# Reordered steps in the pair loop of a hyperbolic attention block: two accumulating transfers issued earlier, one MLP half later, the output add ahead of two PSUM copies

## The reference

```python
x = x + _L1_attn_ref(_layernorm(x, axis=-1), L1_attn_wq, L1_attn_wk, L1_attn_wv, L1_attn_wo)
x = x + _L1_ffn_ref(_layernorm(x, axis=-1), L1_ffn_w1, L1_ffn_b1, L1_ffn_w2, L1_ffn_b2)

# inside _L1_attn_ref, heads of width 8, c = 1
diff_sq = q_norm_sq + k_norm_sq - 2.0 * qk
denom = jnp.maximum((1.0 - c * q_norm_sq) * (1.0 - c * k_norm_sq), 1e-06)
dist = jnp.arccosh(jnp.maximum(1.0 + 2.0 * c * diff_sq / denom, 1.0))
attn = jax.nn.softmax(-dist, axis=-1)

# _L1_ffn_ref
h = jax.nn.relu(jnp.einsum('bsd,dw->bsw', x, w1) + b1)
return jnp.einsum('bsw,wd->bsd', h, w2) + b2
```

## Time and profile before

| | us |
|---|---|
| executions | 2479.14, 2481.09, 2484.28 |
| the profiled execution, its own time | 2479.14 |
| its span in the profile | 2477.0 |
| from the first sum of this stage (1364.0) to the end | 1113 |
| clock of TensorE, mean over the span | 0.879 of full |

### The profile page before, as it was taken

The page is one execution under the profiler, slowest core; times in us unless marked ns, Lnnn a source line. Parts: engine busy times, 40 slices in busy tenths (PEclk is TensorE's granted clock), DMA queues, the critical chain, the costliest instruction groups (busy, mean ns, idle before and its releaser), DMA issues. The chain is left out here.

```text
span 2477.0 us, 50064 instructions
## 1 busy us (share of the span) xinstructions
PE 2029.9 (82%) x15066; PEld 1513.2 (61%) x15066; DVE 1956.0 (79%) x5939; ACT 1767.8 (71%) x3085; POOL 1626.4 (66%) x1866
## 2 busy tenths in 40 slices
PE   4999999999999997999995766766777676776776
PEld 4677777777777766888883444544444444444445
DVE  4677776777767766787776899999999999999982
ACT  2666666666667654444422899999999999999985
POOL 2766676676667730000004989999999999999992
PEclk7999999999999997999996578788887878878886
DMA  5000000000000003534530776666766667766674
GB/s 141 1 2 2 2 1 2 2 1 2 1 2 1 1 1 75 120 84 91 117 70 10 136 136 125 121 120 127 140 129 119 119 122 140 139 118 120 119 133 79
DMA packets 81386, 184.22 MB, mean 74 GB/s; under 512 B 9478, under 2 KB 31529, under 8 KB 81194
## 3 DMA queue, kind: packets, MB, share of 16 engines
q0 software_dynamic: 36864, 134.23, 28.8%
q1 hardware_dynamic: 36010, 43.38, 7.8%
q10 hardware_dynamic: 8320, 4.19, 0.7%
HBM read 42.85 MB, written 4.72 MB: 19 GB/s over the span
## 5 line engine op out<-in xcount | busy, mean ns | idle before, releaser
L1551 POOL TENSOR_TENSOR spare<-spare,u 128x1024 f32<-128x1024 f32 x192 | 455.7, 2374 | 16.0
L542 ACT ACTIVATE prob<-s_ps,nmax 128x128 f32<-128x128 f32 (+1 forms) x1024 | 364.4, 432 | 132.2 <-DVE nmax L599 132.2
L599 DVE CUSTOM_DVE_ANT_0 s_ps<-s_ps,mask 128x128 f32<-128x128 f32 (+1 forms) x1024 | 340.7, 385 | 100.7 <-issue 76.4
L1373 PE MATMUL d_ps<-rowsT 28*128 28x256 f32 x1024 | 150.4, 371 | 252.2 <-DVE u L1631 251.6
L579 POOL TENSOR_TENSOR g_lo<-g_all,g_hi 128x512 fp32r<-128x512 f32 x256 | 329.2, 1286 | 21.4
L1627 DVE TENSOR_SCALAR u<-d_ps 128x1024 f32<-128x1024 f32 x256 | 312.0, 1219 | 37.8 <-PE i_ps L1373 36.7
L1631 DVE SCALAR_TENSOR_TENSOR u<-i_ps,u 128x1024 f32<-128x1024 f32 x256 | 313.5, 1225 | 13.2 <-DVE u L1627 0.5
L1373 PEld LDWEIGHTS d_ps<-rowsT 28*128 28x128 f32 x1024 | 97.0, 219 | 340.8 <-issue 329.3
L534 ACT COPY g_all<-g_ps 128x512 f32<-128x512 f32 x256 | 151.5, 592 | 162.6 <-PE g_ps L63 161.5
L1508 ACT ACTIVATE u<-u 128x1024 f32<-128x1024 f32 x256 | 256.6, 1056 | 0.3 <-DMA u<-spare 0.3
L1511 ACT ACTIVATE u<-u 128x1024 f32<-128x1024 f32 x256 | 255.7, 1051 | 0.0
(11 more groups left out here) (273 smaller groups left out, 5621.9 us busy)
## 6 DMA issues: line engine op xcount, KB each, us to landing
u<-spare POOLq DMA_DIRECT2D x256, 512.0 KB, 12.2
w_all<-w_rows SPq DMA_DIRECT2D x128, 256.0 KB, 5.9
x<-L_attn_x ACTq DMA_DIRECT2D x8, 512.0 KB, 13.9
y<-x SPq DMA_DIRECT2D x32, 128.0 KB, 9.9
wkqv<-L_attn_Wkqv SPq DMA_DIRECT2D x4, 528.0 KB, 8.8
gate_rows<-L_ffn_gate_proj SPq DMA_DIRECT2D x1, 512.0 KB, 14.3
up_rows<-L_ffn_up_proj SPq DMA_DIRECT2D x1, 512.0 KB, 11.4
down_cols<-L_ffn_down_proj SPq DMA_DIRECT2D x1, 512.0 KB, 13.2
```

The lines of the kernel that those rows point to most:

```text
L542: last = nc.scalar.activation(prob[:, kind, at, :].rearrange("p c n -> p (c n)"), s_ps[kind][:, at.start * P:at.stop * P], ACT.Exp, bias=n ...
L599: last = nc.vector.tensor_tensor_reduce(out=scores, in0=scores, in1=keep.mask[:, N - width:N], scale=-1.0, scalar=3.4e38, op0=ALU.add, op1 ...
L1373: last = nc.tensor.matmul(ps[:, e * W2 + j * N:e * W2 + (j + 1) * N], rowsT[at, slot(i, p), 1, j * P:(j + 1) * P], rowsT[at, slot(i, p), 0 ...
L1551: nc.gpsimd.tensor_tensor(extra, extra, pair, ALU.mult).then_inc(prod_done, 1)
```

## The change

Three moves; nothing is added or removed.

1. `SUMS_BEHIND`: GpSimd issues the sums of pairs 0 and 1 behind product 4, ahead of product 5, and the other six behind product 5 as before.
2. `HIDDEN_AT`: the first half of `pe_hidden` moves on TensorE from the end of p = 1 to p = 2, behind the pairs of p = 3 and ahead of the values. The second half keeps its place at p = 3.
3. VectorE, p = 1: `dve_y` stands ahead of the copies of rows 5 and 6 instead of behind them.

```diff
-    SUMS_BEHIND = {5: (0, 1, 2, 3, 4, 5, 6, 7)}
+    SUMS_BEHIND = {4: (0, 1), 5: (2, 3, 4, 5, 6, 7)}
...
-    HIDDEN_AT = (1, 3)
+    HIDDEN_AT = (2, 3)
...
-                        if four_before and p == HIDDEN_AT[1]:
-                            pe_hidden(pe, b - 4, 1, (b + 1) * (HP // 2))
+                        if four_before and p in HIDDEN_AT:
+                            if not one_after:
+                                pe.wait_ge(late_xT4_done, 1)
+                            pe_hidden(pe, b - 4, HIDDEN_AT.index(p), (b + 1) * (HP // 2))
                         if one_before and p in VALUES_AT:
                             pe_values(pe, b - 1, VALUES_AT.index(p), (i - 1) % TURN)
...
                         if five_before and p == 0:
                             pe_y(pe, b - 5, 2 * (b - 1))
-                        if four_before and p == HIDDEN_AT[0]:
-                            if not one_after:
-                                pe.wait_ge(late_xT4_done, 1)
-                            pe_hidden(pe, b - 4, 0, (b + 1) * (HP // 2))
...
                         dve_ratio(dve, b, p, i)
                         if p == 0 and three_before:
                             dve_residual(dve, b - 3)
+                        if p == 1 and five_before:
+                            dve_y(dve, b - 5)
                         for r in {0: (4,), 1: (5, 6), 2: (7,)}.get(p, ()):
                             copy_rows(dve, b, r, i)
-                        if p == 1 and five_before:
-                            dve_y(dve, b - 5)
```

## The result

The changed kernel takes 2571.15 us (median of 4 executions, 2565.5 to 2571.97), the kernel before 2480.11 us in the same comparison (4 executions, 2477.56 to 2484.28). The ratio is 1.0361 [1.0339, 1.0382]: 91 us slower. I had predicted 2510 us, with a range up to 2545. The profiled execution took 2562.97 us, its span is 2560.8.

What follows compares the result with a forecast made beforehand. VectorE's in-order program was taken as the chain, with ScalarE and GpSimd nearly full too. Move 3's 26.9 us plus Move 1's 1.8 in the tail made 28.7, so 2507.8 on the profiled execution, stated as 2510 us; range 2485 to 2545.

Steps and rivals of the forecast that it cites:

- So at full clock it costs the pairs nothing: TensorE ahead of the pairs of p = 4: 1.30 us of idle time covers the moved half's 1.03, leaving 0.27.
- 26.9 for the add: VectorE, `dve_y` ahead of the copies: 13 batches at 1.14 us plus 14 at 0.86 us later, 26.9 us in all.
- the 0.86 us that I gave it: VectorE's next pair in a batch without a wait at L1672: 1646.72 against 1645.86, 0.86 us later through Move 3.
- the second kind: Batches where VectorE's add of y starts without waiting for `pe_y`; 14 of 27, each forecast 0.86 us later.
- the first kind: Batches where VectorE waits at L1672 for `pe_y` before the add; 13 of 27, each forecast 1.14 us later.
- nothing comes of it: Rival: the delay falls into VectorE's waits of 0.59 and 1.11 us, leaving 0 to 2 us; 2482 us, chance 0.08.
- I find no absorption: VectorE's later waits for `i_ps` and the turned output shift with its own pairs, so they take back none of Move 3's delay.
- bounds up to 21 us: Move 1 in the body: loss at most about 1.5 us for each of 14 second-kind batches, 21 us; a gain excluded.
- The slack of 0.2 us ahead of `pe_turn_x4`: `pool_norm4` on GpSimd ends at 1641.7, TensorE wants it at 1641.95: 0.2 us left where there were 1.7.
- In the tail I had 1.8 us: Tail, Move 1: root 5 on ScalarE starts about 1.8 us later, at about 2421.8, without cover.
- well under 0.83: Sign in the changed kernel's profile: TensorE's granted clock in the stage well under 0.83 would point to the first rival.
- the first rival: TensorE's clock falls in the 2.8 us gap ahead of p = 3's pairs; 35 us more, 2545 us, chance 0.2.

Runs made afterwards that it cites:

- the gap filled: Moves 2 and 3 on the kernel before, first half of `pe_hidden` also computed at its old place at p = 1, result overwritten: 2490.20 us, 1.0057.
- both fillings: First half of `pe_hidden` also at its old place, six constant matmuls ahead of the third `pe_values` at p = 4: Moves 2, 3 2474.28 us; all three 2523.36 us.
- all three, gap filled: The changed kernel with the first half of `pe_hidden` also computed at its old place at p = 1, result overwritten: 2538.93 us, 1.0245 against the kernel before.
- the same, `pool_norm4` earlier: All three moves, first half of `pe_hidden` also at its old place, `pool_norm4` directly behind sum 2 instead of sum 5: 2516.77 us, 1.0151 against the kernel before.

## Why the prediction was wrong

**The direction was right, the size was not.** I predicted 2510 us, 29 us slower, and got 2571, 91 us slower.

**The step that failed is Move 2, "So at full clock it costs the pairs nothing", costed at 0.** The condition was the error. At full clock the sentence holds: with the gap filled, 0.24 us of idle time is left ahead of the pairs of p = 4, where I had 0.27. I had worked out the gap ahead of the pairs of p = 3 as 2.8 us (measured 2.42) and the delay behind it as 2.7 us (in the batch shown, a wait of 2.82), and then left both out of the sum, as a rival with a chance of 0.2 that bites in half of the batches. It bites in 23 of 27, half of them at about 1.7 us and half at about 2.9. Its term is 47 us. With it the sum is 2507.8 + 47 = 2555. The rest is the wait of L1672, which grew by 36.6 us where the sum had 26.9 for the add: 2565, against 2562.97 for the profiled execution. The gap came out shorter than 2.8 us because Move 3 widened it less than the 0.86 us that I gave it: alone it leaves 1.18 to 1.35 us there, from 0.54 to 0.90. I had also read the 0.90 us of the second kind as that of both; the first kind has about 0.63.

**Move 3.** Alone it costs 7 us and not 26.9; my "nothing comes of it" rival was nearer to that run than my sum. This is so since the kinds of batch are no property of the kernel and the wait at L1643 shrank. "I find no absorption" is wrong there. It is wrong with both fillings too, where Moves 2 and 3 cost 25 us: the wait at the add is 38 us longer, more than my term, and 15 us of it come back at the turned output. That 25 and 26.9 agree is in part luck.

**Move 1.** In the body I costed it at 0 and gave bounds up to 21 us. Alone it costs 8. The slack of 0.2 us ahead of `pe_turn_x4` does not hold once VectorE stands directly behind `pe_y`: with Move 3 it costs 29 us, 48 with Moves 2 and 3 and the gap filled, and 50 with both fillings, all above my bound of 21. In the changed kernel most of this falls into the wait for `i_ps`. In the tail I had 1.8 us and measured 0.4.

**What the profile was to show.** Seen: L1672 waits in all 27 batches; the half of L1436 at p = 2; the sums two at a time ahead of product 5; root 5 waiting for L1551 and L1479 for L1349, as these rows of the changed kernel show:

```profile
1682.67 1.80 POOL L1541 DMA_DIRECT2D u<-spare  x2 [5.16 <-ACT spare L1495]
...
1684.18 0.52 POOL L1548 TENSOR_TENSOR spare<-u,twos 128x4 f32<-128x4 f32 x1
```
```profile
1688.18 1.06 ACT L1495 ACTIVATE spare<-spare 128x1024 f32<-128x1024 f32 x1 [1.55 <-POOL spare L1551]
```
```profile
1670.16 0.38 ACT L1479 ACTIVATE rows<-misc 128x256 fp32r<-128x256 f32 x1 [3.49 <-PE misc L1349]
```

Not as written: L1479 waits 3.49 us there and not 1.4, the instances lie 37.33 us apart and not 35.1, the waits of L1672 are 46.6 us and not 35, and the granted clock is 0.73, "well under 0.83", the sign that I had named for the first rival. A sign for it stood in the rows of before: at 0.83 in the stage the clock was falling already, without the longer gap.

## What to carry to other kernels

When a move takes work off TensorE at one place, look at the gap that it leaves and at what stands behind the gap: 1 us of work in each batch, moved from one side of a wait to the other, cost 16 us here alone, and 88 in company of a move that cost 7 alone. Put a computed gap and a computed delay into the sum, not among the rivals, when the stage's mean clock shows that the clock falls already. And sum moves only after asking which of them use the same slack; three that cost 8, 16 and 7 us alone cost 91 together.

## What the runs showed of the hardware

Extra matmuls that nobody reads made a kernel faster at two places: 2476.48 to 2447.46 us at p = 4, and 2564.31 to 2490.20 in the gap.

The idle time ahead of the pairs of p = 3, and how many of 27 blocks behind it ran at 1.2 GHz in whole or in part:

| kernel | idle time, us | slow blocks |
|---|---|---|
| before | 0.54 to 0.90, once 1.51 | 0 |
| Move 3; Moves 1, 3; Moves 2, 3, gap filled | 1.18 to 1.35 | 0 |
| all three, gap filled | 1.18 to 1.35 | 15 |
| the same, `pool_norm4` earlier | 1.18 to 1.35 | 5 |
| Moves 1, 2 | 1.40 to 1.59, once 2.60 | 4 |
| Move 2 | 1.41 to 1.77, once 2.68 | 16 |
| all three | 2.41 to 2.42 | 24 |
| Moves 2, 3 | 2.41 to 2.42 | 27 |

So the widest gap goes with the most slow blocks, but one and the same gap goes with none, 5 or 15, and no run shows which of the earlier steps of the batch makes that difference.

Two issues of accumulating transfers of 512 KB took 1.80 us of GpSimd, 0.90 each, as the six of before took 0.89 each. A root takes ScalarE 0.945 us, so an issue holds its engine nearly as long.
